# Where the first experts' rows are gathered: a graph transformer kernel whose first mixture of experts adds its gated rows into the result tensor in memory

## What is computed

```
xn = layernorm(x)
x = x + gnn0(xn) + attention0(xn)
# first mixture of experts: 8 experts, each token goes to its best 2
xf = layernorm(x)
probs = softmax(xf @ router_w.T + router_b)
top_probs, expert_ids = top_k(probs, 2)
w = top_probs / (sum(top_probs) + 1e-9)
y = xf @ expert_w[e].T + expert_b[e]          # for the two e of each token
x = x + w[0] * y[expert_ids[0]] + w[1] * y[expert_ids[1]]
# second layer
xn = layernorm(x)
x = x + gnn1(xn) + attention1(xn)
x = x + second mixture of experts (two matrices with a gelu between them)
```

## Time and profile before

| | |
|---|---|
| median of 3 runs (lowest, highest) | 1882.05 us (1880.01, 1882.09) |
| the profiled execution's own time | 1882.65 us |
| its span in the trace | 1880.7 us (1.95 us lie around it) |
| busy: PE / DVE / ACT / POOL | 94% / 39% / 21% / 7% |
| share of the chain that ended last: PE / DVE / DMA | 84% / 8% / 2% |
| graph attention of layer 0 | to about 731 us |
| ranking for the first experts | about 740 to 757 us |
| first experts, 25 tiles | 763 to 974 us |
| next attention's first projection | from 1000 us |

### The profile page before, as it was taken

One profiled execution on the slowest core, in us unless ns is written; L12 is line 12 of the kernel. 1 busy time (PEld: TensorE's weight loads), 2 busy tenths in 40 slices (PEclk: granted clock), 3 DMA queues, 4 the chain that ended last, 5 costly groups with the idle time before them and its releaser, 6 DMA issues.

```text
span 1880.7 us, 24731 instructions
## 1 busy us (share of the span) xinstructions
PE 1769.1 (94%) x7994; PEld 1090.2 (58%) x7995; DVE 725.2 (39%) x1826; ACT 392.5 (21%) x1034; POOL 134.1 (7%) x169
## 2 busy tenths in 40 slices
PE   7999999999999986899997999999999999779997
PEld 4555555554333343566666855555569669756664
DVE  4321545756789887211116211151111114432222
ACT  2441221113322222011013321000221221122221
POOL 0000000000000000111114000000000000013322
PEclk9999999999999998899998999999999999879999
DMA  6001101001001114355536011010010012535772
GB/s 196 1 0 62 68 24 39 1 1 36 30 23 49 34 42 182 95 200 190 195 130 190 30 51 51 0 51 0 0 51 1 0 50 84 193 105 139 198 196 40
DMA packets 53582, 142.22 MB, mean 76 GB/s; under 512 B 10079, under 2 KB 20723, under 8 KB 53045
## 3 DMA queue, kind: packets, MB, share of 16 engines
q1 hardware_dynamic: 34053, 87.05, 13.4%
q0 software_dynamic: 11952, 34.05, 7.5%
q10 hardware_dynamic: 7488, 19.93, 3.0%
HBM read 113.69 MB, written 33.99 MB: 79 GB/s over the span
## 4 chain that ended last, share of the span: by engine, by line
PE 84%; DVE 8%; issue 2%; DMA 2%; DVEq 2%; ACT 1%; ACTq 0%; POOL 0%; SPq 0%; POOLq 0%
PE PS L734 21%; PE PS L1076 10%; PE PS L744 8%; PE PS L1186 5%; PE PS L1208 5%; PE PS L842 4%; PE PS L876 4%; PE PS L1158 4%; PE PS L1144 4%; PE PS L1117 4%; PE PS L982 3%; DVE WRA L1867 3%; PE PS L823 2%; PE PS L1054 2%; PE PS L991 2%
## 5 line engine op out<-in xcount | busy, mean ns | idle before, releaser
L734 PE MATMUL PS<-WS,XT 128*125 128x384 f32 x960 | 313.6, 488 | 1.4 <-issue 1.4
L734 PEld LDWEIGHTS PS<-WS,XT 128*125 128x125 f32 x960 | 180.5, 189 | 129.5 <-issue 3.6
L1076 PE MATMUL PS<-WS,XGT 128*128 x600 | 199.4, 490 | 0.0
L1076 PEld LDWEIGHTS PS<-WS,XGT 128*128 128x128 f32 x600 | 113.1, 192 | 74.4 <-issue 2.0
L744 PE MATMUL PS<-XT,WS 128*128 128x416 f32 (+1 forms) x432 | 151.2, 512 | 0.0
L1867 DVE SCALAR_TENSOR_TENSOR WRA<-RB,U,AT 125x500 f32<-125x500 f32 (+1 forms) x240 | 140.0, 645 | 2.2 <-PE PS L991 0.6
L744 PEld LDWEIGHTS PS<-XT,WS 128*128 128x128 f32 x432 | 81.6, 189 | 69.2 <-issue 69.2
L982 PE MATMUL PS<-WRA,F 125*64 125x500 f32 (+1 forms) x480 | 100.7, 531 | 9.7 <-DVE WRA L1867 8.6
L1186 PE MATMUL PS<-WS,XGT 128*128 x288 | 99.4, 496 | 1.5 <-ACTq L1406 1.1
L2011 DVE TENSOR_TENSOR YS<-PS,EBB 128x768 f32<-128x768 f32 x25 | 23.9, 957 | 191.2 <-PE PS L1076 191.2
L1208 PE MATMUL PS<-WS,HT 128*128 x276 | 92.9, 486 | 1.0 <-DVE YS L2005 1.0
(11 more groups left out here) (319 smaller groups left out, 2149.6 us busy)
## 6 DMA issues: line engine op xcount, KB each, us to landing
WS<-in_ewT SPq DMA_DIRECT2D x8, 2304.0 KB, 10.6
WS<-in_fW SPq DMA_DIRECT2D x16, 1152.0 KB, 6.8
WS<-in_w SPq DMA_DIRECT2D x5, 2304.0 KB, 10.5
expert_rows<-YS ACTq DMA_DIRECT2D x25, 384.0 KB, 2.3
xn_rows<-XN ACTq DMA_DIRECT2D x20, 336.0 KB
RB<-expert_rows SPq DMA_DIRECT2D x12, 488.3 KB
WS<-in_wp SPq DMA_DIRECT2D x2, 2304.0 KB, 8.3
WS<-in_W SPq DMA_DIRECT2D x2, 2304.0 KB, 8.7
```

The lines of the kernel that those rows point to most:

```text
L734: last = nc.tensor.matmul(ps[0:T, 0:HC], lhsT[:, k, t * T:(t + 1) * T], w[:, k, b * HC:(b + 1) * HC], start=(k == 0), stop=(k == KC - 1))
L1076: last = nc.tensor.matmul(PS[:, 4 + 2 * a + b, 0:HC], XGT[:, a, k, :], WS[:, bass.ds(slot, 1), k * C + b * HC:k * C + (b + 1) * HC].rearra ...
```

## The change

The first mixture takes the way of the second. SyncE stores the ten tiles of `X` into `out_x`, tile 0 to 7 during the graph attention and tiles 8 and 9 behind the first expert matrices and bias rows. VectorE forms three bfloat16 parts of the gates behind the ranking (`gate_terms`), TensorE orders them with 20 matmuls between tile 0 and tile 1 (`gate_products`), and VectorE adds the parts up (`gate_rows`). TensorE then waits for `gates_in` before tile 1, since the products' bank of PSUM is one that tile 1 writes. Each tile's bias row is scaled by the gate into `YS`, the product is scaled and added, and GpSimd adds `YS` into `out_x`. When the last add has landed, SyncE loads `X` back from `out_x` in 20 DMAs (two a tile, one semaphore a tile), and VectorE takes each tile's statistics as it arrives. Gone are the 25 stores to `expert_rows`, the fill of its spare rows from x (3456 KB, early in the program), the 20 gathers and the 20 weighted sums. The first two tiles are written out ahead of the loop, which now starts at 1.

```diff
@@ SyncE
-        spare = 2 * N // P * P
-        sp.dma_start(y_d[spare:, :], x[0:ET_MAX * P - spare, :]).then_inc(y_cleared, 16)
+        def rows_out(t):
+            sp.dma_start(out[t * T:t * T + PA, :], X[0:PA, t, :]).then_inc(acc_in, 16)
+            sp.dma_start(out[t * T + PA:(t + 1) * T, :], X[PA:T, t, :]).then_inc(acc_in, 16)
...
+            if u - 4 in LN1_IN:
+                sp.wait_ge(xn_ready, NT + LN1_IN[u - 4] + 1)
+                rows_out(LN1_IN[u - 4])
...
         sp.dma_start(EBB1, eb.partition_broadcast(P)).then_inc(eb_in, 16)
+        for t in range(LATE, NT):
+            sp.wait_ge(xn_ready, NT + t + 1)
+            rows_out(t)
         expert_loads(1, U_EW, U_MIX1)
+
+        sp.wait_ge(acc_in, 32 * NT)
+        sp.wait_ge(y_all, 1)
+        for t in range(NT):
+            sp.dma_start(X[0:PA, t, :], out[t * T:t * T + PA, :]).then_inc(x2_in[t], 16)
+            sp.dma_start(X[PA:T, t, :], out[t * T + PA:(t + 1) * T, :]).then_inc(x2_in[t], 16)
@@ GpSimd
-        for q in range(KT):
-            if q >= YB[1]:
-                pool.wait_ge(yg_used, q - YB[1] + 1)
-            nc.gpsimd.indirect_dma_start(out=YG1[:, q % YB[1], :], out_offset=None, in_=y_d,
-                                         in_offset=bass.IndirectOffsetOnAxis(ap=IDXA[:, q:q + 1], axis=0)
-                                         ).then_inc(yg_in[q % YB[1]], 16)
...
+        pool.wait_ge(gates_in, 1)
+        pool.wait_ge(acc_in, 32 * NT)
+        add_rows(1, 0, 0, [])
+        pool.wait_ge(turned_n[1], 4)
+        gather(1, 4, 0)
+        add_rows(1, 1, 1, [(0, 1)])
+        with nc.gpsimd.Fori(1, n) as i:
+            pool.wait_ge(turned_n[1], i * 2 + 3)
+            gather(1, i * 2 + 3, 1)
+            add_rows(1, i * 2, 0, [(1, i)])
+            pool.wait_ge(turned_n[1], i * 2 + 4)
+            gather(1, i * 2 + 4, 0)
+            add_rows(1, i * 2 + 1, 1, [(0, i + 1)])
@@ TensorE
+        turn(1, 1, 1, 16)
+        expert0(0, 0)
+        gate_products(1)
+        turn(1, 2, 0, 32)
+        pe.wait_ge(gates_in, 1)
+        expert0(1, 1)
+        with nc.tensor.Fori(1, turns1) as i:
@@ ScalarE
-            act.wait_ge(y_free[1], n + 3)
-            act.dma_start(y_d[bass.ds(n * P, P), :], YS[:, a, :]).then_inc(ys_out[1][a], 16)
@@ VectorE
-            dve.wait_ge(y_filled[L], n + 2)
-            dve.wait_ge(ys_out[L][a], i * 16 + 16)
-            V.tensor_tensor(YS[:, a, :].rearrange("p (b c) -> p b c", b=2), PS[:, b0:b0 + 2, 0:HC],
-                            EBB[L][:, bass.ds(e, 1), :].rearrange("p a (b c) -> p (a b) c", b=2), ALU.add).then_inc(y_free[L], 1)
...
         for t in range(NT):
-            weighted(t, 0)
-            V.drain()
-            weighted(t, 1)
-            if t >= 3:
+            if t:
                 normal(2, t - 1)
-            V.drain()
+            dve.wait_ge(x2_in[t], 32)
             spread_of(2, t)
-            if t == 1:
-                normal(2, 0)
-                normal(2, 1)
```

More of the change, by code:

```diff
@@ L77 @@
 QC = [(o, 250) for o in range(0, N, 250)]
-YB = {1: 4}
 class Jobs:
@@ L669, in add_rows @@
                                          in_=YS[:, a, :], in_offset=None, bounds_check=N - 1, oob_is_err=False,
-                                         compute_op=ALU.add).then_inc(ys_out[3][a], 16)
+                                         compute_op=ALU.add).then_inc(ys_out[L][a], 16)
+        pool.wait_ge(turned_n[1], 2)
+        gather(1, 2, 0)
+        pool.wait_ge(turned_n[1], 3)
+        gather(1, 3, 1)
+        pool.wait_ge(gates_in, 1)
[11 more added lines that the diff above has]
+            add_rows(1, i * 2 + 1, 1, [(0, i + 1)])
+        with nc.gpsimd.Fori(0, over) as j:
+            pool.wait_ge(turned_n[1], n * 2 + j + 2)
+            pool.wait_ge(xg_in[1][0], (n + j) * 16 + 32)
+            gather(1, n * 2 + j + 1, 0)
+            add_rows(1, n * 2 + j, 0, [(1, n), (0, n + j)])
+        pool.wait_ge(xg_in[1][0], (n + over) * 16 + 32)
+        pool.wait_ge(xg_in[1][1], n * 16 + 16)
+        pool.wait_ge(ys_out[1][0], (n + over) * 16)
+        pool.wait_ge(ys_out[1][1], n * 16)
+        nc.gpsimd.sem_inc(y_all, 1)
         def gather3(k, b):
@@ L1055, in turn, with gate_products @@
             last.then_inc(turned_n[L], 1)
+        def gate_products(k):
+            pe.wait_ge(gate_parts, k)
+            tvg = TVG[1 if k == 1 else 3]
+            for q in range(KT):
+                last = nc.tensor.matmul(PS[:, 7, 0:4 * ETC], OHR[:, q, :], tvg[:, q, :, :].rearrange("p a b -> p (a b)"),
+                                        start=(q == 0), stop=(q == KT - 1))
+            last.then_inc(gates_full, 1)
         def weights_of(L, n, u0):
@@ L1218, in _ @@
         hidden(0, 0)
-        pe.wait_ge(gate_parts, 1)
-        for q in range(KT):
-            last = nc.tensor.matmul(PS[:, 7, 0:4 * ETC], OHR[:, q, :], TVG[:, q, :, :].rearrange("p a b -> p (a b)"),
-                                    start=(q == 0), stop=(q == KT - 1))
-        last.then_inc(gates_full, 1)
+        gate_products(2)
         with nc.tensor.Fori(0, turns3) as i:
@@ new lines, in expert_rows @@
+            if not isinstance(i, int):
+                dve.wait_ge(ys_out[L][a], i * 16)
+            V.tensor_scalar(YS[:, a, :], EBB[L][:, bass.ds(e, 1), :].rearrange("p a c -> p (a c)"), gate, None, ALU.mult)
+            V.tensor_copy(SX[:, a:a + 1], SIDX[:, bass.ds(n, 1)])
+            V.drain()
+            dve.wait_ge(y_filled[L], n + 2)
+            ys = YS[:, a, :].rearrange("p (b c) -> p b c", b=2)
+            V.scalar_tensor_tensor(out=ys, in0=PS[:, b0:b0 + 2, 0:HC], scalar=gate, in1=ys, op0=ALU.mult,
+                                   op1=ALU.add).then_inc(y_free[L], 1)
@@ new lines, in expert_rows, with gate_terms @@
+            V.drain().then_inc(ys_ready[L], 1)
+        def gate_terms(tvg):
+            V.drain()
+            V.tensor_copy(GPB[:, 0], GW)
+            V.drain()
+            V.tensor_tensor(GR, GW, GPB[:, 0], ALU.subtract)
+            V.drain()
+            V.tensor_copy(GPB[:, 1], GR)
+            V.drain()
+            V.tensor_tensor(GR, GR, GPB[:, 1], ALU.subtract)
+            V.drain()
+            V.tensor_copy(GPB[:, 2], GR)
+            V.drain()
+            terms = tvg.rearrange("p (t k) v e -> p t k v e", k=2)
+            for n in range(2):
+                ot = OT.rearrange("p (t k) e -> p t k e", k=2)[:, :, n, :]
+                for m in range(3):
+                    V.tensor_tensor(terms[:, :, n, m, :], ot, GPB[:, m, n, :].unsqueeze(2).to_broadcast([T, NT, ETC]), ALU.mult)
+            V.tensor_copy(tvg[:, :, 3, :], OT)
+            V.drain().then_inc(gate_parts, 1)
@@ L2020, in _ @@
+        V.drain()
         V.drain()
         route(1, 1, True)
+        gate_terms(TVG[1])
         dve.wait_ge(eb_in, 16)
@@ L2024, in _ @@
         over1 = nc.vector.value_load(TAB[0:1, 2, 1:2], min_val=1, max_val=2)
-        with nc.vector.Fori(0, turns1) as i:
+        gate_rows(1)
+        for a in range(2):
+            expert_rows(1, a, a, 0)
+        with nc.vector.Fori(1, turns1) as i:
             for a in range(2):
```

135 lines of the change are left out of this document (42 added, 93 removed).

## The result

The changed kernel is slower: 1890.92 us median of 5 runs (1890.25 to 1893.77) against 1882.05 (1880.01 to 1883.88), a ratio of 1.0051, 95% interval 1.0038 to 1.0063. Forecast were 1876.2 us and a range of 1872.6 to 1880.8.

A forecast was written before the change was run, and what follows sets the result against it. TensorE was taken as the bound, with one 26.4 us hole between last sum and projection. Tail gain 8.45 less front loss 2.5 gave about 5.9 us, hence 1876.2 us, range 1872.6 to 1880.8 for 8 in 10.

The forecast's parts named there:

- For the index work ahead of it I allow 1.4 ... 4.0 of 8.40.: Expert loop: GpSimd's gather issue, index work and add issue take 4.0 us of each 8.40 us tile.
- the 7.5 us of slack: Expert loop: a gather behind an add lands by 17.0 us, while TensorE wants it at 24.5, leaving 7.5 us.
- Nothing holds it: GpSimd's last gather came a tile earlier.: Tail: GpSimd starts issuing the last add 0.97 us after the last sum ends, with nothing holding it.
- ScalarE's square root of the degrees ... is out of the way.: Tail: the degree root comes straight behind the degree sums at 984.46, clear of tile 0's normalisation ending at 987.4.
- The other terms of the tail: Last sum to projection: add landing 5.6 us, hop 0.15, load 2.8, statistics 1.54, among others; tail gain 8.45 us.
- The front: Between tile 0 and tile 1: gate matmuls 1.22 us plus a gate wait of 1.25, 2.5 us lost (1.7 to 3.3).
- The fill: Early in the program: the spare rows' fill was off the path, so removing it was costed at nothing.
- The adds bound the loop: Rival, expert loop: each add waits for the one before; landings above 8.96 us lose time, 1895 at 9.5; 6%.
- Slow loads: Rival, tail: X's queued loads come back slowly, 7.4 us for tile 0, gain falls by 4.6 to 1880.8 us; 14%.
- The clock does not fall: Rival, tail: TensorE's clock stays up in the shorter hole before the projection, 3.5 us more gained, 1872.7; 8%.
- The "DVE blocks DMA" trap (SWDGE): Expert loop: by this rule VectorE's bias row scaling blocks GpSimd's descriptor writing and would stretch the add's issue; no size given.

The follow-up runs named there:

- experiments 1 to 3: Changed kernel with indices made by VectorE, 1870.9 us; with semaphores for GpSimd's two drains, 1872.08; the first plus one drain before each gather, 1884.0.
- experiment 1: Changed kernel with VectorE making the first mixture's gather indices, so GpSimd has no index work or drains between add and gather: 1870.9 us, ratio to before 0.9945.
- experiment 7: Side by side: changed kernel with VectorE's indices, 1872.58 us; the same plus gate products in bank 3 and tile 0's root before the degree root, 1868.45 us.
- experiment 8: Changed kernel with the 3456 KB fill of the spare rows put back: 1895.13 us, beside 1891.6 us for the changed kernel on the same chip.

## Why the prediction was wrong

- **"For the index work ahead of it I allow 1.4 ... 4.0 of 8.40."** This step failed. I took GpSimd's step as the sum of its instructions, 4.0 us, and in it stood the two drains as they are with nothing outstanding, 0.36 and 0.25. The drain ends only when the add has landed. From an add's issue to the cast passed 5.65 and 7.95 us in the rows above, and behind it come 0.2, 0.8, 1.0 and 0.3 up to the next add: a row of 7.95 us a tile in one case and of 10.25 in the other. From the add's issue to the gather's it was 7.2 us at the median, where my sum had 3.0, so more than half of the 7.5 us of slack was gone at once; and with a mean row of 8.94 against TensorE's 8.40 the rest followed and the late landings held TensorE. 24 steps of 0.54 make 13.1 us, the +13.2 of this stage; experiments 1 to 3 show the cause. The kernel before had a row that said it: the maximum of its own drain, 3784 ns against a median of 360, behind the only index work that followed close on a gather. The second mixture, which I took as the model for the adds, has its indices made by VectorE and no drain, and so could not show it.
- **"Nothing holds it: GpSimd's last gather came a tile earlier."** Failed, and by more than the drains. The spare tile's gather stands between the last two adds. With its drains it held the last add, +1.3 us, and TensorE's transposes ahead of the degree sums, 6.36. Without drains the add is free (2.15 behind the sum's start, forecast 1.99), but the gather is still late for TensorE, 2.30 (experiment 1).
- **"ScalarE's square root of the degrees ... is out of the way."** Failed in its premise, that the degree sums end where they did, 10.4 us behind the start of the last sum. Without the drains they end 14.8 behind it (experiment 1: 987.02 - 972.18): TensorE waits for the spare gather, and the first sums then take 7.35 us in place of 5.97, with a granted clock of 0.66 from 975 to 980. The degree root behind them comes later than tile 0's statistics and stands ahead of tile 0's root on ScalarE. From the statistics' start to the end of `XN` it is 988.51 - 983.39 = 5.12 us, where I had 2.80: 2.3 us lost. With the root ahead it is 2.73 (experiment 7). That an earlier spare gather alone would do the same is likely, but no run tried it.
- **The other terms of the tail** held, once these two were gone: 18.75 us against 18.3 (experiment 7). From the sum's start to the add's issue 2.15 (forecast 1.99); from there to SyncE's first load 5.41 (5.75); the load, to the statistics, 3.64 (2.8). The load is the term that was mis-sized, by 0.84. The rule of the Trainium skill on a fixed 2.0 us and bytes over 436 GB/s ("DMA: Bandwidth & Descriptors", "Anatomy of one DMA — SWDGE (gpsimd) path"), by which I estimated 2.9 for an add, is not borne out: the median was 5.6 to 5.9.
- **The front** cost 3.55 - 0.66 = 2.9 us between tile 0 and tile 1, where the forecast had 2.5: its wait was put at 1.25 and is 1.67. The term that was too small is the reading of the expert number with its register work, 0.6 in my sum: it begins at 770.7 and the matmuls at 771.87. 1.4 of the 2.9 came back by luck, since tile 0's matmuls took 8.26 us in place of 9.66, in a better clock that I had not forecast.
- **The fill** I counted as off the path. It wasn't: taking it out gained some 3.5 us (experiment 8) and hid part of the loss; 2.0 of the 3.0 us in the table's first row stand already behind the key-value sums (195.36 against 197.32). The profile of before had the pause, 2.44 us under "issue", which I passed over as nobody waited for the fill.
- **Rivals.** *The adds bound the loop* named the right place and the right side, at 6 in a hundred, with the wrong mechanism: with the drains gone, adds that land in 5.7 us (at most 9.1) cost the loop nothing. *Slow loads* held in part, 0.84 of 4.6. *The clock does not fall* was wrong: the clock was 0.50 from 990 to 995 in the changed kernel, and also in the short tail of experiment 7, 0.50 from 980 to 985, where the first 36 records of the projection took 9.61 us (10.41 before). The other rule of the Trainium skill, 'The "DVE blocks DMA" trap (SWDGE)' of the page "SBUF — State Buffer", left hardly a mark: in experiment 1 the add's issue takes 1.59 us also where VectorE's scaling of the bias row begins 0.05 us ahead of it, and in the changed kernel 1.60, at most 1.74 where the scaling begins 0.35 us ahead.
- **Left over:** 1.4 us less behind the projection's start than before. In the profiles of the twelve experiments this stage is 874.5 to 879.8 us long, so I make nothing of it.

## What to carry to other kernels

When a transfer is put onto an engine's queue, list all that the engine does behind it, and ask of each drain what is outstanding at that moment; a semaphore raised by the one instruction that matters orders just as well and does not wait for transfers. A drain's minimum and maximum by line, not its mean, show it in the old profile. When a new instruction is put onto a queue, follow also what it pushes back, down to work that seems harmless: the spare tile's gather feeds nothing, but TensorE waited for it, and behind that stood the degree sums, the degree root and the root that the next stage needed.

## What the runs showed of the hardware

- A drain on GpSimd behind an accumulating indirect DMA of 384 KB lasted 6.1 to 6.2 us at the median (9.6 to 9.8 at most), until some 0.3 us behind the DMA's landing, which took 5.8 to 5.9; GpSimd's own compute in the same place, ordered by a semaphore, started at once. With nothing outstanding the drain took 0.36, the small product ahead of it included.
- The small product on GpSimd took 0.77 us where it started while an add's issue was still running, and 0.18 to 0.19 where it did not (983.61 in the changed kernel; the kernel before).
- A background DMA of 3456 KB that nobody waits for went with one pause of TensorE of 2.4 to 2.8 us, between two of the 240 key-value matmuls, and cost some 3.5 us. The profile puts it under "issue".
- TensorE's granted clock rose earlier at tile 0 in the changed kernel (0.75 from 760 to 762 us, then 1.00) than in the one before (0.50 until 766). Tile 0 took 7.93 to 8.45 us in the changed kernel and all its variants, 8.02 with the fill put back, and 9.66 to 9.83 in the kernel before and its variants. The cause is open.
- With an add in flight a gather of 384 KB landed 5.5 us after its issue at the median (experiment 1), as against 4.1 in the changed kernel, where a gather goes out 1.3 us ahead of its add and not 1.9 behind. It cost the loop nothing.
